# A Mamba-style scan and a mixture of experts: another order of a scan slot, products made one stage earlier, a fifth product on GpSimd

## What is computed

```
x      = silu(conv(in_proj(ctx)) + conv_b)          # u
dt     = softplus(dt_proj(dt_low) + dt_b)
state  = state * exp(dt * A) + (dt * u) * B         # 16 states for each channel
y      = sum over the 16 states of state * C
y      = (y + D * u) * silu(layernorm(x_in))
x1     = x_in + y
out    = x1 + moe(layernorm(x1)) + shared(layernorm(x1))   # top 2 of 16 experts, width 352
```

## Time and profile before

| | us |
|---|---|
| median of 3 runs (lowest, highest) | 1085.01 (1083.24, 1085.73) |
| the profiled execution | 1088.87 |
| its span in the trace | 1087.1 |
| first stage, to the first scan | 0 to 105.65 |
| slots 0 to 3, no shared expert | to about 203 |
| slots 4 to 15, with it | to 606.6 |
| to the loop over the experts, and that loop | to 1087.1 |

### The profile page before, as it was taken

How to read it: one execution, slowest core, us unless ns; L and a number is a source line. 1 busy time by engine, 2 the same in 40 slices (tenths; PEclk the granted TensorE clock), 3 DMA queues, 4 the chain that set the end, 5 groups by cost and what they waited for, 6 DMA issues and landing times.

```text
span 1087.1 us, 16598 instructions
## 1 busy us (share of the span) xinstructions
PE 913.7 (84%) x4352; PEld 671.4 (62%) x4353; DVE 831.9 (77%) x1349; ACT 515.1 (47%) x959; POOL 753.9 (69%) x482
## 2 busy tenths in 40 slices
PE   5876555778889888878998899969998999998993
PEld 2222344556556556656665555639997988897992
DVE  4788999989998899988999413869888987989000
ACT  3777634544554555455555222115554545554541
POOL 3437888988888888878994200026887888887872
PEclk9996656789999899989999989989999999999996
DMA  5469821651237322552210230036676866774432
GB/s 191 181 240 338 290 87 49 229 216 49 69 103 295 107 77 77 202 214 87 64 52 29 78 128 11 20 110 190 158 210 166 235 167 184 193 221 107 77 58 39
DMA packets 69987, 152.14 MB, mean 140 GB/s; under 512 B 7585, under 2 KB 23969, under 8 KB 64306
## 3 DMA queue, kind: packets, MB, share of 16 engines
q1 hardware_dynamic: 59410, 126.97, 33.8%
q0 software_dynamic: 10528, 24.65, 11.4%
HBM read 112.80 MB, written 38.80 MB: 139 GB/s over the span
## 4 chain that ended last, share of the span: by engine, by line
PE 51%; DVE 25%; issue 14%; ACT 4%; POOL 2%; DMA 2%; DVEq 1%; ACTq 0%; SPq 0%; POOLq 0%
PE bank L665 11%; PE bank L684 8%; PE bank L611 7%; PE bank L769 6%; PE bank L771 6%; PE bank L770 6%; DVE bank L1344 5%; DVE gs L1358 4%; DVE p_acc L1286 2%; DVE e_gu_lo L1571 2%; DVE e_gu_hi L1570 2%; DVE bank L1563 2%; ACT bank L925 1%; PE bank L758 1%; PE bank L553 1%
## 5 line engine op out<-in xcount | busy, mean ns | idle before, releaser
L1151 POOL TENSOR_TENSOR dbu<-bcs,m_w 128x2048 f32<-128x2048 f32 x64 | 295.1, 4613 | 29.0 <-DVE bank L1344 25.9
L925 ACT ACTIVATE bank<-m_dt,c_a 128x512 f32<-128x512 f32 x256 | 171.3, 685 | 235.2 <-DVE gs L1358 235.2
L1344 DVE TENSOR_TENSOR_SCAN bank<-bank,dbu 128x512 f32<-128x512 f32 x192 | 230.8, 1219 | 16.5 <-ACT bank L925 15.6
L665 PE MATMUL bank<-ws_gu,f_xnT 128*128 128x352 f32 x576 | 204.8, 499 | 31.5 <-ACT f_hT L947 29.7
L611 PE MATMUL bank<-ident,gs 128*128 128x128 f32 x768 | 141.5, 320 | 57.3 <-DVE gs L1358 50.3
L611 PEld LDWEIGHTS bank<-ident,gs 128*128 128x128 f32 x768 | 107.4, 164 | 115.6 <-DVE gs L1358 71.0
L665 PEld LDWEIGHTS bank<-ws_gu,f_xnT 128*128 128x128 f32 x576 | 112.4, 208 | 82.1 <-ACT f_hT L947 30.9
L769 PE MATMUL bank<-e_gu_hi,e_xT_hi 128*128 x376 | 130.0, 346 | 8.1 <-POOL e_xT_lo L1216 5.4
L1358 DVE TENSOR_TENSOR gs<-bank,bcs 128x512 f32<-128x512 f32 x192 | 128.3, 669 | 0.0
L771 PE MATMUL bank<-e_gu_hi,e_xT_lo 128*128 x376 | 121.9, 324 | 0.0
L770 PE MATMUL bank<-e_gu_lo,e_xT_hi 128*128 x376 | 121.8, 324 | 0.0
(11 more groups left out here) (166 smaller groups left out, 1680.9 us busy)
## 6 DMA issues: line engine op xcount, KB each, us to landing
bcs<-bc_scratch SPq DMA_DIRECT2D x32, 1024.0 KB, 9.1
e_gu<-in_wgu SPq DMA_DIRECT2D x16, 1408.0 KB
e_dn<-in_wdn SPq DMA_DIRECT2D x16, 512.0 KB
out_rows<-xt SPq DMA_DIRECT2D x18, 256.0 KB, 2.1
p_x<-in_x SPq DMA_DIRECT2D x4, 1024.0 KB, 6.8
u_scratch<-p_u SPq DMA_DIRECT2D x4, 1024.0 KB, 3.9
silu_z_scratch<-p_sz SPq DMA_DIRECT2D x4, 1024.0 KB, 5.0
dt_scratch<-p_dt SPq DMA_DIRECT2D x4, 1024.0 KB, 4.8
```

The lines of the kernel that those rows point to most:

```text
L665: last = mm(dst[:, 0:I], lhs[t], ws_gu[:, t, off:off + I], start=t == 0, stop=t == KH - 1)
L925: f(HS[k % RING_H][:], m_dt[:, q % 2, :], ACT.Exp, scale=c_a[:, q, n:n + 1]).then_inc(exp_done, 1)
L1151: g.tensor_tensor(part_, Bs[:, gr * GRP:(gr + 1) * GRP, :], w, ALU.mult).then_inc(dbu_ready, 1)
L1344: v.tensor_tensor_scan(to, h, dbu[:, n, :], 0.0, ALU.mult, ALU.add).then_inc(scan_done, 1)
```

## The change

It does five things.

1. The products w = dt * u are made in the first stage by GpSimd (`products`, four for each batch), stored to `w_scratch` (`w_store`, 1 MB for each batch) and loaded for each slot into one of two buffers `m_w` (256 KB, between dt and u). The product at the start of each slot goes. Batches 0 and 1 are made before the layer norms of batches 2 and 3; those of batch 2 stand in GpSimd's list between groups 1 and 2 of slot 0, those of batch 3 after each group of slot 2.
2. u has two buffers in the first stage, and new waits: ScalarE's `silu_u` and VectorE's `soft` wait for products that still read u or dt; `clear` in slot 2 waits for the stores of u and w; the load of C's last group for batch 0 waits for three w stores, since their source lies there.
3. GpSimd makes five products with C, for the states (1), (5), (8, 10), (13), grouped so; VectorE makes eleven. `ORDER` is changed to suit.
4. The positions in a slot are others: three early pieces before the first sum instead of one, the rest spread to position 10; late pieces spread too; `gate` at 6 and 8 instead of both at 9; `hT_copy` at 2 instead of 4; `hidden` at 9 and 13 instead of 12 and 15; `swish` after group 0 instead of 1.
5. Buffer bookkeeping (`in_same_buffer`) for counts that the ring does not divide.

```diff
-POOL_N = (1, 5, 9, 13)
+POOL_GROUPS = ((1,), (5,), (8, 10), (13,))
+POOL_N = sum(POOL_GROUPS, ())
-ORDER = (0, 2, 3, 1, 4, 6, 7, 5, 8, 10, 11, 9, 12, 14, 15, 13)
+ORDER = (0, 2, 3, 1, 4, 6, 7, 5, 9, 11, 8, 12, 10, 14, 15, 13)
-SWISH_AFTER = 1
+SWISH_AFTER = 0
-PE_AT = (1, 1, 2, 4, 4, 4, 4, 5, 5, 5, 6, 8, 8, 8, 8, 9, 10)
-LATE_AT = (0, 0, 0, 0, 1, 2, 3, 4, 5, 6, 6, 6, 6, 6, 6, 6, 6)
+PE_AT = (3, 3, 4, 4, 5, 5, 6, 6, 7, 7, 8, 8, 9, 9, 9, 10, 10)
+LATE_AT = (0, 0, 0, 1, 1, 2, 2, 3, 3, 5, 5, 6, 6, 6, 6, 6, 6)
-GATE_AT, HT_AT, XN_AT, XNT_AT = 9, 4, (14, 10), (15, 15)
-TAKE_AT, LOGITS_AT, GATED_AT, HIDDEN_AT, STATS_AT, ADD_AT = 2, 5, 4, (12, 15), (8, 1), 15
+GATE_AT, HT_AT, XN_AT, XNT_AT = (6, 8), 2, (14, 10), (15, 15)
+TAKE_AT, LOGITS_AT, GATED_AT, HIDDEN_AT, STATS_AT, ADD_AT = 2, 5, 4, (9, 13), (8, 1), 15
...
+def in_same_buffer(at, ring, count):
+    return at + ring * ((count - 1 - at) // ring)
...
+            def w_store(b):
+                sp.wait_ge(w_made, b * DT + DT)
+                sp.dma_start(w_d[b:b + 1].rearrange("a p t l -> p (a t) l"), p_w[b]).then_inc(w_stored, 16)
...
+                sp.dma_start(m_w[par][:, 0, :], w_d[bass.ds(b, 1), :, q, :].rearrange("a p l -> p (a l)")).then_inc(w_loaded[par], 16)
...
             load_bc(0, 2, 1)
+            w_store(2)
+            sp.wait_ge(w_stored, 48)
             load_bc(0, 3, 1)
...
-                    sp.wait_ge(w_ready, i)
+                    sp.wait_ge(dbu_ready, i * NG)
...
-                wait(act, u_stored, b * 16)
+                wait(act, u_stored, (b - 1) * 16)
+                    wait(act, w_made, (b - 2) * DT + q + 1)
...
-            for b in range(B):
-                normalise(b)
+            def products(b, q):
+                pool.wait_ge(dt_ready, b * DT + q + 1)
+                if b < B - 1:
+                    wait(pool, w_stored, b * 16)
+                g.tensor_tensor(p_w[b][:, q, :], p_dt[:, q, :], p_u[b % 2][:, q, :], ALU.mult).then_inc(w_made, 1)
+
+            normalise(0)
+            normalise(1)
+            for b in range(B - 2):
+                for q in range(DT):
+                    products(b, q)
+                normalise(b + 2)
...
-                g.tensor_tensor(m_w[:, 0, :], m_u[:, q % 2, :], m_dt[:, q % 2, :], ALU.mult).then_inc(w_ready, 1)
-                pool.wait_ge(w_ready, i + 1)
+                pool.wait_ge(w_loaded[q % 2], b * 32 + (q // 2) * 16 + 16)
...
+                        for n in POOL_GROUPS[gr]:
+                            times_c(*((b, q - 1) if q else (b - 1, DT - 1)), n)
...
+                    if isinstance(b, int) and i == 0 and gr == 1:
+                        for k in range(DT):
+                            products(B - 2, k)
+                    if isinstance(b, int) and b == 0 and q == 2:
+                        products(B - 1, gr)
...
                 dve.wait_ge(bc_stored, 16 * B)
+                dve.wait_ge(u_stored, 16 * B)
+                dve.wait_ge(w_stored, 16 * B)
                 v.memset(xt[:, 2:4, :], 0.0)
```

More of the change, by code:

```diff
@@ L281, in program @@
          out_stored, trash_stored, rt_max, rt_exp, rt_mask, rt_rank, rt_oh, rt_table,
-         tables_ready) = [s[n] for n in names[at:at + 44]]
+         tables_ready) = [s[n] for n in names[at:at + 43]]
         xt_loaded = [xt0_loaded, xt1_loaded, xt2_loaded, xt3_loaded]
@@ L385, in _ @@
             load_x(3)
+            w_store(0)
             load_bc(0, 1, 0)
@@ L441, in slot @@
                     sp.wait_ge(exp_done, i * NS)
-                    sp.wait_ge(w_ready, i)
+                    held(sp)
+                    sp.wait_ge(dbu_ready, i * NG)
+                    held(sp)
                     sp.wait_ge(du_ready, i)
@@ L481, in _ @@
                 sp.dma_start(xn_d[t * P:(t + 1) * P, :], f_xnT[:, 2, :]).then_inc(trash_stored, 16)
-            for stored in (u_stored, bc_stored, dt_stored, sz_stored):
+            for stored in (u_stored, bc_stored, dt_stored, sz_stored, w_stored):
                 sp.wait_ge(stored, 16 * B)
@@ L572, in x_dbl @@
                     pe.wait_ge(u_ready, b * DT + q + 1)
-                    last = mm(XDB[0:NX, :], p_xp[:, q, :], p_u[:, q, :], start=q == 0, stop=q == DT - 1)
+                    last = mm(XDB[0:NX, :], p_xp[:, q, :], p_u[b % 2][:, q, :], start=q == 0, stop=q == DT - 1)
                 last.then_inc(xd_ready, 1)
@@ L627, in y_sum @@
                     pe.wait_ge(g_ready, i * NV + by_vector(n) + 1)
-                    tile = gs[:, (q * NV + by_vector(n)) % RING_G, :]
+                    tile = gs[:, by_vector(n) % RING_G, :]
                 add_turned(tile, m == 0, m == NS - 1).then_inc(ymm_done, 1)
@@ L987, in slot @@
                         hT_copy(j, 1)
-                    if n == GATE_AT:
-                        for c in range(2):
-                            if rows:
-                                gate((j[0] + 1, (q + 1) % TB), c)
-                            elif q == DT - 1:
-                                gate((0, 0), c)
+                    if n in GATE_AT:
+                        c = GATE_AT.index(n)
+                        if rows:
+                            gate((j[0] + 1, (q + 1) % TB), c)
+                        elif q == DT - 1:
+                            gate((0, 0), c)
                     if rows and n == XN_AT[q > 0]:
@@ L1164, in times_c @@
                 if not (isinstance(i, int) and i == 0 and at < RING_P):
-                    j, m = (i, POOL_N[at - RING_P]) if at >= RING_P else (i - 1, POOL_N[at - RING_P + NP])
+                    j, m = (i, POOL_N[at - RING_P]) if at >= RING_P else (i - 1, POOL_N[in_same_buffer(at, RING_P, NP)])
                     pool.wait_ge(ymm_done, j * NS + ORDER.index(m) + 1)
@@ L1292, in soft @@
                 wait(dve, dt_stored, b * 16)
+                wait(dve, w_made, (b - 1) * DT + q + 1)
                 v.scalar_tensor_tensor(p_dt[:, q, :], DTP[q][:], 0.0, p_e[:, q, :], ALU.max, ALU.add).then_inc(sum_ready, 1)
@@ L1341, in scan @@
                     if not (isinstance(i, int) and i == 0 and at < RING_P):
-                        dve.wait_ge(gp_ready, i * NP + at - RING_P + 1)
+                        dve.wait_ge(gp_ready, i * NP + at - RING_P + 1 if at >= RING_P else (i - 1) * NP + in_same_buffer(at, RING_P, NP) + 1)
                     to = h_p[:, at % RING_P, :]
@@ L1348, in times_c @@
                 dve.wait_ge(scan_done, b * STEPS + k + 1)
-                if n % GRP == 0:
+                if all(m // GRP < n // GRP for m in DVE_N if m < n):
                     dve.wait_ge(c_loaded[n // GRP], b * 16 + 16)
```

43 lines of the change are left out of this document (22 added, 21 removed).

## The result

The changed kernel takes 1073.41 us (median of 4 runs, 1072.0 to 1074.58) against 1085.26 for the kernel before (4 runs): a ratio of 0.9894, 95% interval 0.9876 to 0.9911. It is faster, by 11.9 us, which is under half of the 25.6 us forecast. So windows of the two profiled executions show a difference about 5 us larger than the medians do.

A forecast was written before the change was run, and what follows sets the result against it. No engine fills the 30.89 us slot; a ring of waits between VectorE and TensorE sets it. Slots 4 to 15 -26.6, slots 0 to 3 0, first stage +1.0: -25.6 from 1085.0, 1059.4 us, range 1049 to 1077.

The forecast's parts named there:

- the ring of the ordinary slot: Ordinary slot of 30.89 us: TensorE and VectorE wait for each other in series, 20.2 and 10.7 us; no engine fills it.
- the rival that gives half of it back at GpSimd and ScalarE: Slots 4 to 15: GpSimd's gate waits and ScalarE leave ordinary slots at 29.9, about 1075 us; chance 0.20.
- Positions: Ordinary slot: earlier pieces remove VectorE's 1.85 us wait at hidden; VectorE's list 28.0, slot 28.6 us with later waits.
- scan 13: Ordinary slot: VectorE waits for GpSimd's product 8 to free an h_p buffer, priced at 0.3 us.
- scan 0: End of slot: last down piece and ScalarE's copies delay the next decay, cost 0.2 to 0.6 us, taken as 0.3.
- Fifth product: Each slot: VectorE gives up one product with C, saving 0.59 us; GpSimd gains 1.28, loses w's 1.27, list 27.2.
- 8 us if it decided alone: Skill's rule against products on GpSimd: 0.7 us a slot, some 8 us in all, unless GpSimd's slack absorbs it.
- Slot 0: Batch 2's four GpSimd products fill a 3.01 us pause; group 2 ends near 121, wanted about 125; cost 0.
- slot 2: Four more GpSimd products delay slot 1's product 13: +1.2 us; clearing waits for the last w store: 0.6 us.
- First slot of a batch: Slots 4, 8, 12: the extra over an ordinary slot, 1.84 before, is left at 1.8, giving 30.4 us each.
- Last slot of a batch: Slots 7, 11 and 15: counted among the nine ordinary slots at 28.6 us, without a term of their own.
- First stage: Before the first scan: an added store and two loads delay GpSimd's first group, +1.0 us, between 0 and +4.

The follow-up runs named there:

- e6: Kernel before with the new positions alone: w in the slot, four GpSimd products, old order of sums; ratio 0.9772 to the kernel before, 1057.9 us.
- e3: Changed kernel, w made early, but four GpSimd products and the old order of sums; ratio 0.9785 to the kernel before, 1058.0 us.
- e10: Changed kernel with B and C loads of batches 1 to 3 cut to one partition, so computed with batch 0's; ratio 0.9846 to the kernel before.
- e5: Changed kernel once more, unaltered; ratio 0.9885 to the kernel before, 1070.8 us.
- e4: Kernel before with only w made early, stored and loaded; old positions, old order, four products; ratio 1.0003 to the kernel before, 1082.8 us.
- e2: Kernel before with new positions, new order and fifth GpSimd product, w still made in the slot; ratio 0.9830 to the kernel before, 1063.4 us.
- e7: e6 with VectorE's loop over batches written out; ratio 0.9720 to the kernel before, 1052.7 us.
- e1: Changed kernel with VectorE's loop over batches 1 to 3 written out; ratio 0.9819 to the kernel before, 1061.3 us.
- e11: Kernel before with VectorE's loop over batches written out; ratio 0.9940 to the kernel before, 1077.3 us.
- e8: Changed kernel with B's first group loaded ahead of dt, w and u at batch ends; ratio 0.9887 to the kernel before, 1071.0 us.
- e9: e2 with three buffers for h_p instead of two; ratio 0.9783 to the kernel before, 1060.6 us.
- e12: e7 with the second tile's statistics at position 10 instead of 8, norm's root after group 2; ratio 0.9812 to the kernel before, 1063.3 us.

## Why the size of the prediction was wrong

The direction was right, and what breaks the ring of the ordinary slot too. The gain was 11.9 us instead of 25.6, near the 1075 of the rival that gives half of it back at GpSimd and ScalarE, though not by the longer ordinary slots from which that rival was worked out.

**Positions: right.** The prediction broke the ring at `hidden`, put an ordinary slot at 28.6 and found 28.40. The sum is nearer than its terms, which is in part luck. From start to start VectorE's own list came to 27.7, not 28.0. Its waits were 0.11 us before scan 13, where GpSimd's product of state 8 had just ended (0.3 forecast), 0.36 before scan 0 (0.3 forecast) and 0.23 before `hidden` of half 1 (none forecast). TensorE had no pause over 1.1 us left before an early piece, its wait for the copy came to 4.7 us between 216 and 561 us, and it ran at a granted clock of 1.00 in the slot against 0.94: the full 2.4 GHz level. The Trainium skill (TensorE: Matmul & The Clock Gate, What's actually happening) has sustained activity release the throttle; the trace agrees, with 26.24 us of TensorE's work for 133 instructions where it was 27.32. e6 shows that these edits alone hold the gain.

**Fifth product: the step that failed.** The prediction credited it with 0.59 us a slot on VectorE, put GpSimd's list at "27.15 + 0.01 = 27.2" and saw slack in that. The list is right (27.10 busy in slot 10), and neither number was the question. With twelve products VectorE is busy for 28.06 us of a slot of 28.25 (e3); with eleven the slot is 28.40 long, since the chain over TensorE and ScalarE at its end then comes last. So there was no 0.59 to collect. That this chain is later because of the new order of sums is read from the timelines; no run changed the order alone. In slots 0, 2, 7 and 11 the product is on VectorE's path itself, through the two buffers of `h_p`: 5.2, 1.5, 2.0 and 1.2 us of waits, none of them in e3 (those of slots 7 and 11 also go when the loads there are small, e10). The product takes 1286 ns on GpSimd over the whole run against 667 on VectorE:

```profile
L1394 DVE TENSOR_TENSOR gs<-bank,bcs 128x512 f32<-128x512 f32 x176 | 116.0, 667 | 0.0
L1202 POOL TENSOR_TENSOR g_p<-h_p,bcs 128x512 f32<-128x512 f32 x80 | 101.9, 1286 | 16.9 <-DMA m_w<-w_scratch 7.0
```

The prediction priced this at 8 us if it decided alone, and set that aside on GpSimd's slack. Fifth product and early w together cost 12 us (e5 against e6), early w without the fifth product nothing (e4), or 0.1 point (e3 against e6), and the fifth product without early w 0.6 points (e2 against e6). That the two together cost more than their sum is at the edge of the noise in the ratios; slot 0 shows it in the windows, with `h_p` waits of 5.2 us for both, 0.6 for the fifth product alone (e2) and none for early w alone (e3). The Trainium skill (GPSIMD Engine Reference, 4.1 Engine selection) keeps such products on VectorE, and the runs agree, in the ratio of the two durations (1.9) and in effect: the kernels with the product on VectorE are faster by 0.6 to 1.1 points.

**Slot 0: 0 forecast, 2.6 measured.** I compared batch 2's four products with the deadline of group 2, that is, with `dbu`, which has three groups of lead. The queue on the same engine also holds the products with C, and behind them stands a ring of two `h_p` buffers with no lead. That is where VectorE waited: 1.98 and 3.19 us. In slot 2 I did price this ring, at 1.2, and found 1.52; the clearing's wait, put at 0.6, was 0.90. With four products both `h_p` waits are absent (e3, slot 0 at 42.2).

**First slot of a batch: 30.4 forecast, 32.2 to 33.0 measured.** The prediction took the difference 32.73 - 30.89 = 1.84 as this slot's price and added it to the new slot. That difference was net. The slot has a second set of statistics (1.15, from 417.15 to 418.30 in the ordinary slot's one set) and waits for the tile through HBM (1.79), together 2.9; before, the ring's waits were shorter in that slot (1.11 us at `hidden` and none for the decay, against 1.85 and 0.42 in the ordinary one) and hid part of it. With the ring gone they count in full: 28.40 + 2.94 = 31.3, and e3 measured 31.2 to 31.5, e7 30.7 to 32.0. The rest is 0.72 more at the slot's end (1.00 against 0.28 for ScalarE's decay, behind the copy of the turned norm) and up to 1.3 at `hidden`. Both are absent in e3 and e6, with four products; in e7's slot 8 there is one wait for the decay, 0.69. Over three slots 7.0 us are missed.

**Last slot of a batch: 28.6 forecast, 34.1 and 32.4 measured.** I took it for an ordinary one. Its 1.85 us before VectorE's first scan of the next batch stood in the trace of before under ScalarE's name:

```profile
354.29 1.23 DVE L1344 TENSOR_TENSOR_SCAN bank<-bank,dbu 128x512 f32<-128x512 f32 x1 [1.85 <-ACT bank L925]
```

where other slots have 0.42. That was the loop's return, and it is the same step of the program that takes 5.32 and 4.47 us now. DMA queues between 350 and 356 us, before and after (packets, MB, share of the engines):

```profile
q1 hardware_dynamic: 415, 1.55, 66.1%
q14 instruction: 1, 0.01, 0.4%
```

```profile
q1 hardware_dynamic: 496, 1.97, 96.6%
q14 instruction: 1, 0.01, 0.3%
```

VectorE stopped at 352.44 before and at 349.60 after. One packet of the instruction queue, 8 KB, began between 352.0 and 352.5 before and between 352.5 and 353.0 after (a view of that half microsecond), and VectorE went on at 354.29 and 354.92. So before, the packet began as VectorE got there; after, VectorE was there 3 us ahead of it. In e10 one began between 347.5 and 348.0, where VectorE stopped at 347.70 and went on at 349.92. From such a packet to VectorE's next scan it is about 2 us in all three; what differs is the time before it begins. In the changed kernel the loads of the next batch filled just that time:

```profile
349.50:352.50 3.00, 2.64 (x21) 2.03 (x19) 0.10 (x1) 2.78 (x5) 3.00 (x3) 1.00 1.05 395
```

The DMA share is 1.05 there, against 0.54 in the same 3 us of the kernel before. These are loads of C and two stores; w for the next slot is issued only at 352.92, and without early w the return takes 4.71 us too (e6). The Trainium skill (Runtime: NRT & Kernel Launch, Instruction fetch mechanics) says that a taken branch out of the buffered code forces a fetch by DMA before execution goes on; the trace agrees in that packet, and in 0.91 us without the branch. The record does not say for which engine a packet was, but with VectorE's loop alone written out (e1, e7, e11) no instruction packet begins between 340 and 360 us. One more packet began earlier in both kernels, between 349.0 and 349.5 before and between 348.5 and 349.0 after; what it brought is not shown. With the two waits for `h_p` (0.77 and 1.19, in slot 7), less the statistics that this window lacks, slot 7 comes out: 28.40 - 1.15 - 0.28 - 0.16 + 0.77 + 1.19 + 5.32 = 34.1. The two slots miss the forecast by 9.2 us, and slot 15 is 4.0 under it, since its window is a short one (27.6 before) that the sum took for an ordinary one.

**First stage: +1.0 forecast, +0.4 measured.** This tells little: the first scan lies between 104.8 and 106.7 over all kernels, 104.8 in one with early w (e3). The sum behind the +1.0 takes 1.25 MB for a store of 1 MB and two loads of 256 KB, which are 1.5 MB and at 334 GB/s over 4.5 us instead of 3.7.

**Open.** What moved the stretch behind the last take by 4.8 us; how much of the twelve us of fifth product and early w falls to the ring of buffers and how much to the new order of sums, which no run tested by itself; and, at the size of medians, how much more the return costs after than before. A third `h_p` buffer in the changed kernel itself was not tried.

## What to carry to other kernels

When a ring of waits is broken, price every special slot from its own gross work and waits, since the difference between it and an ordinary slot was taken while the ring hid part of it. Before work is added to the engine with "slack", check each queue behind it against its shortest ring of buffers, not its longest lead, and ask what the engine it is taken from will then wait for. And where an engine's loop turns round just as the next stage's loads start, a faster engine waits there for its own code: write the loop out.

## What the hardware showed that I had not expected

VectorE's return to the head of its loop took 1.85 and 1.91 us in the kernel before, 3.55 and 2.21 in e4, 3.9 to 5.4 at the first return of the kernels with the new positions (e2 4.35, e3 4.99, e6 4.71, e8 5.42, e9 3.90, after 5.32), 2.22 and 2.46 with small loads (e10), and 0.91 to 0.92, a wait for ScalarE, where it was written out (e1, e7, e11, e12). Three labels stood for it: ScalarE, GpSimd and "issue", as whichever semaphore came last. The other surprise is how little a lighter engine can be worth: with one product less VectorE is busy for 27.74 us instead of 28.06, and the ordinary slot grew from 28.25 to 28.40, since VectorE then waits for TensorE and ScalarE at its end.
